# A different prologue for a one-core kernel: one load of the input, constants in two loads, the weights' low part on VectorE

## The chip, the cores and the metric

The kernel runs on one core of one Trainium2 chip. The metric is the device time of one execution in microseconds (us), as the median of several runs.

## The reference

The input `x` is 8 images of 64 channels of 16x16 pixels in float32. Two blocks follow each other, each added to its input:

```
g = group_norm(x)                              # 32 groups of 2 channels, per image
offsets = conv3x3(g, off_w) + off_b            # 8 heads x 9 taps x 2
aw = sigmoid(conv3x3(g, attn_w) + attn_b)      # 8 heads x 9 taps
v = Wv g
sampled = bilinear(v at pixel + tap + offset)  # 4 corners, zero outside
x = x + Wo * sum_taps(sampled * aw)
h = group_norm(x)
p_gn = group_norm(conv3x3(top_pool(relu(conv3x3(h, p1))) + left_pool(relu(conv3x3(h, p2))), p_w))
x = x + relu(conv3x3(relu(p_gn + group_norm(conv1x1(h, c1_w))), c2_w) + c2_b)
```

Only the start of the first block, up to its offset and attention convolutions and its values, is touched by the change.

## The kernel before

Every engine has a hand-written program that runs in its own order, and semaphores tie them together. The prologue goes like this.

- Loads. SP issues the first four images to `x_b` (partitions 0 to 63), all constants to `cst`, the convolution weights `w_off` to the lower half of `w_raw` (it shares its memory with `prod`, the name that the trace shows), the eight images once more to `x_t` (all eight on partitions 0 to 63), then biases, value weights and small vectors. ACT's queue issues images 4 to 7 to the upper half of `x_b`, and `w_off` to the upper half of `w_raw`.
- Statistics. VectorE (DVE) takes mean and variance of each channel from `x_b` (L586 to L592). TensorE (PE) joins the two channels of a group with two matrices out of `cst` (L917; it waits for the whole of `cst`). DVE makes the variances (L598 to L600), GpSimd (POOL) raises them to the power -0.5 (L374), and DVE makes the shifts (`affine`, L609).
- The normalised input. `g_t` gets the eight images out of `x_t`: five by DVE (L702), three by ScalarE (ACT, L418).
- Splitting. Float32 products are made from rounded parts: `g_pair` holds the rounded input on partitions 0 to 63 and the same, one column on, on 64 to 127; `g_cross` holds the rest of the rounding on the lower half and the rounded input on the upper. This is done in three ranges of columns: DVE writes `g_pair` (L709) and `g_cross` (L711), ACT copies both to the upper half (`copy_high`, L426 and L427). The weights are split in the same way: `w_pair` by DVE (L716, queued behind the first range) and ACT (L432, queued behind the first `copy_high`), `w_cross` by ACT (L412) with its upper half then reduced to the low part by POOL (L382), and the bias row by ACT (L430) and POOL (L387).
- The convolutions. The 16 columns of the image are worked on in chunks of 2, 4, 4, 4 and 2 (`CHUNKS`). `conv_column` makes one column by 6 matmuls of `g_pair` (L958), 9 of `g_cross` (L964), and one for the bias (L966). PE makes chunk 0, then all values (`values`, L939), then chunk 1, and then the rest between its other work. Until its input is there PE is kept busy by 20 matmuls that nobody reads (`keep_warm`, L924), which start behind the statistics.
- Behind it, ACT copies offsets out of PSUM (L449), makes the interpolation weights (`distances`, `hats`), and copies the values out (`copy_values`, L439). DVE multiplies (L768, L733, L760). PE sums (L979, L1004). From chunk 0 on the same pattern repeats for each chunk, and the second block follows.

Of the kernel before, what the change touches and what calls it, by code (L numbers as in the profile page):

```python
# [70 lines left out]
BETWEEN = (3, 2, 2, 0, 0)  # L71
WARM_START, WARM_CHUNK = 20, (0, 0, 0, 16, 10)
WARM_IN = (11, 14)
# [12 lines left out]

C_GB = 0
C_GT = C_GB + P
C_RAMP = C_GT + 2 * P
C_ID = C_RAMP + 2 * W - 1  # L90
# [16 lines left out]
def build(nc, x, consts, w_off, w_v, off_bias, w_o, w12, b12, wp, wc1, wc2, vecs, out):  # L107
    with ExitStack() as ctx:
# [90 lines left out]
        ld_x = [sem(f"ld_x{i}") for i in range(2)]  # L199
        ld_xt = sem("ld_xt")  # L200
        ld_cst = sem("ld_cst")
        ld_w0 = [sem(f"ld_w0_{i}") for i in range(4)]
        ld_w12, ld_wp, ld_vec, ld_c = sem("ld_w12"), sem("ld_wp"), sem("ld_vec"), sem("ld_c")
# [105 lines left out]
        def _(sp):  # L309
            sp.dma_start(x_b[lo, :, :], x_d[0:HALF].rearrange("n c p -> c n p")).then_inc(ld_x[0], 16)  # L310
            sp.dma_start(cst[:, :], consts).then_inc(ld_cst, 16)
            sp.dma_start(w_raw[lo], w_off).then_inc(ld_w0[1], 16)
            sp.dma_start(x_t[:, :, :], x_d.rearrange("n c p -> c n p")).then_inc(ld_xt, 16)
            sp.wait_ge(bias_zero, 1)
            for row in (0, LO_ROW):
                sp.dma_start(bias_s[row:row + 1, :], off_bias).then_inc(ld_w0[2], 16)
            for rows in (lo, hi):
                sp.dma_start(w_v_s[rows, :], w_v).then_inc(ld_w0[0], 16)
            sp.dma_start(w_o_s[:, :], w_o).then_inc(ld_w0[3], 16)
            sp.dma_start(vec_s[:, :], vecs).then_inc(ld_vec, 16)  # L320
            sp.dma_start(b12_s[:, :], b12).then_inc(ld_vec, 16)
# [39 lines left out]
        @block.gpsimd  # L361
        def _(pool):
            nc.gpsimd.memset(ones[:, :], 1.0).then_inc(zeroed, 1)
            nc.gpsimd.memset(bias_s[:, :], 0.0).then_inc(bias_zero, 1)
            nc.gpsimd.memset(half_pow[:, :], -0.5)
            nc.gpsimd.memset(g_pair[:, PW - 1, :, :].bitcast(F32), 0.0)
            nc.gpsimd.memset(ones_r[:, :].bitcast(F32), 1.0)
            nc.gpsimd.memset(w_v_pair[:, :].bitcast(F32), 0.0)
            nc.gpsimd.memset(w_pair[:, 1::2, :].bitcast(F32), 0.0).then_inc(zeroed, 1)
            nc.gpsimd.memset(v[:, :, :, :], 0.0).then_inc(v_zero, 1)  # L370

            def rstd(s, cols):
# [4 lines left out]
            pool.wait_ge(zeroed, 2)  # L377
# [24 lines left out]
        DVE_IMAGES = 5  # L402

        @block.scalar
        def _(act):
# [8 lines left out]
            act.wait_ge(ld_xt, 16)  # L414
            act.wait_ge(g_zero, 1)
            act.wait_ge(norm_ready, 1)
            for n in range(DVE_IMAGES, N):
                nc.scalar.activation(g_t[:, 1:W + 1, 1:H + 1, n].rearrange("p x y -> p y x"), rows_cols(x_t[:, n, :]),  # L418
                                     ACT.Identity, bias=ab[lo, G0, 3, n:n + 1],
                                     scale=ab[lo, G0, 2, n:n + 1]).then_inc(g_ready, 1)  # L420

# [9 lines left out]
            copy_high(0)  # L431
            nc.scalar.activation(w_pair[hi, 0::2, :], w_raw[hi, 1::KS, :], ACT.Copy).then_inc(w_high, 1)  # L432
            copy_high(1)
# [10 lines left out]
            def copy_offsets(c):  # L444
                x0 = CHUNKS[c][0]
                act.wait_ge(off_ps, c + 1)
                for b, k in enumerate(CONV_BANKS[c]):
# [123 lines left out]
        def _(ve):  # L571
# [123 lines left out]
            norm_stats(G0, [x_b[:, n, :] for n in range(HALF)])  # L695
            variance(G0, N, bank[7][:, 0:2 * N])
            affine(G0, N)
            ve.wait_ge(norm_ready, 1)
            ve.wait_ge(ld_xt, 16)
            ve.wait_ge(g_zero, 1)  # L700
            for n in range(DVE_IMAGES):
                nc.vector.tensor_scalar(g_t[:, 1:W + 1, 1:H + 1, n].rearrange("p x y -> p y x"),  # L702
                                        rows_cols(x_t[:, n, :]), ab[lo, G0, 2, n:n + 1], ab[lo, G0, 3, n:n + 1],
                                        ALU.mult, ALU.add).then_inc(g_ready, 1)

            ve.wait_ge(g_ready, N)
            ve.wait_ge(zeroed, 2)
            for r, (xa, xb) in enumerate(RANGES):
# [201 lines left out]
        def _(pe):  # L910
# [33 lines left out]

            def conv_column(c, j):

# [6 lines left out]
                if c and j == (2 if c == 1 else 0):  # L953
                    pe.wait_ge(u_ready, c)
                ps = bank[CONV_BANKS[c][j // 2]][:, (j % 2) * NCH:(j % 2 + 1) * NCH]
                for t in range(2 * KS):
                    ky, single = t // 2, t % 2
                    nc.tensor.matmul(ps, g_pair[:, x + 2 * single, ky:ky + H, :].rearrange("p y n -> p (y n)"),  # L958
                                     w_pair[:, t, :], start=(t == 0), stop=False)
                if c == 0 and j == 0:  # L960
                    pe.wait_ge(w_split, 2)
                for t in range(K2):
                    ky, kx = t // KS, t % KS
                    nc.tensor.matmul(ps, g_cross[:, x + kx, ky:ky + H, :].rearrange("p y n -> p (y n)"),  # L964
                                     w_cross[:, t, :], start=False, stop=False)
                last = nc.tensor.matmul(ps, ones_r[:, :], bias_r[:, :], start=False, stop=True)  # L966
                if j == CHUNKS[c][1] - 1:
                    last.then_inc(off_ps, 1)

            def tap_sum(c, g):  # L970
# [62 lines left out]
            pe.wait_ge(v_ready, 1)  # L1033
# [156 lines left out]
```

## Time and profile before

| | |
|---|---|
| median of 3 runs | 163.49 us (161.29 to 163.99) |
| the profiled execution's own time | 164.37 us |
| its span, first to last instruction | 162.5 us |
| mean granted TensorE clock, as a share of 2.4 GHz | 0.964 |
| busy: PE, DVE, ACT, POOL | 80%, 69%, 36%, 14% of the span |
| chain that ended last: PE, DVE, issue, DMA, ACT | 48%, 26%, 10%, 7%, 5% |

The profile's first line of each engine gives its busy share, and the chain of work that ended last says which of that work set the end. An engine may be busy and off that chain. The span leaves out 1.87 us of the execution's own time (164.37 less 162.5).

### The profile page before, as it was taken

Reading aid. Unit: us, or ns where it says so; the run is one execution under the profiler, and the core shown is the slowest. Engines: PE = TensorE matmul, PEld = TensorE weight load, DVE = VectorE, ACT = ScalarE, POOL = GpSimd, SP = SyncE. Lnnn points to the kernel's source line nnn. Section 1 sums busy time; section 2 is a strip of 40 time slices with the busy share of each in tenths; the row PEclk is TensorE's granted clock in tenths of the full one; section 3 lists DMA queues with packets and bytes.
Section 4 is the critical chain, followed back from the end, with each engine's and each line's share of the span. In section 5 each row is a group of like instructions: output and inputs, shape, how many; then the busy total and the mean of one; then the engine's idle time right before and its main releaser. Section 6 shows DMA issues by size and latency. Waiting matters only on the chain.

```text
span 162.5 us, 3252 instructions
## 1 busy us (share of the span) xinstructions
PE 130.0 (80%) x1387; PEld 110.9 (68%) x1387; DVE 112.7 (69%) x195; ACT 59.2 (36%) x107; POOL 22.4 (14%) x27
## 2 busy tenths in 40 slices
PE   0069109999899899999999998998689996685790
PEld 0057009999799789999899886886476564453560
DVE  5515997059148999699969999985580596857611
ACT  3009058660990469007962054020010415103301
POOL 8817900000000000000035000000010101020100
PEclk9999955999999999999999999999978999999998
DMA  4991000009963000000000000000000000000014
GB/s 127 246 188 28 0 0 0 4 0 257 237 128 78 0 2 4 0 0 4 0 0 0 4 0 0 0 0 6 2 0 4 0 6 4 0 4 0 0 36 97
DMA packets 7058, 5.96 MB, mean 37 GB/s; under 512 B 4656, under 2 KB 6194, under 8 KB 7042
## 3 DMA queue, kind: packets, MB, share of 16 engines
q1 hardware_dynamic: 6370, 4.71, 12.6%
q10 hardware_dynamic: 672, 1.02, 2.5%
q8 instruction: 11, 0.18, 0.5%
q14 instruction: 5, 0.04, 0.1%
HBM read 3.31 MB, written 0.52 MB: 24 GB/s over the span
## 4 chain that ended last, share of the span: by engine, by line
PE 48%; DVE 26%; issue 10%; DMA 7%; ACT 5%; SPq 1%; POOL 1%; POOLq 0%; DVEq 0%
PE bank L964 9%; PE bank L979 9%; PE bank L1004 7%; PE bank L958 7%; DMA x_t<-in_x 7%; DVE prod L733 6%; PE bank L924 4%; DVE part L760 3%; DVE x_t L859 3%; PE bank L1095 3%; PE bank L1128 3%; PE bank L939 2%; DVE wy L768 2%; DVE g_t L702 2%; DVE pooled L865 1%
## 5 line engine op out<-in xcount | busy, mean ns | idle before, releaser
L760 DVE TENSOR_TENSOR part<-v,bank 128x1280 f32<-128x1280 f32 (+3 forms) x20 | 21.5, 1111 | 9.7 <-PE bank L1004 4.3
L733 DVE TENSOR_TENSOR prod<-hat,wy 128x1440 f32<-128x1440 f32 (+3 forms) x25 | 27.3, 1158 | 0.0
L979 PE MATMUL bank<-cst,prod 128*128 128x128 f32 (+3 forms) x189 | 22.3, 272 | 0.8 <-DVE prod L733 0.8
L979 PEld LDWEIGHTS bank<-cst,prod 128*128 128x128 f32 (+3 forms) x189 | 20.7, 132 | 1.4 <-DVE prod L733 1.0
L1004 PE MATMUL bank<-cst,part 128*128 128x128 f32 x168 | 20.9, 274 | 0.8 <-issue 0.4
L924 PE MATMUL bank<-ones_r 128*128 128x512 f32 x71 | 20.8, 452 | 0.0
L958 PE MATMUL bank<-w_pair,g_pair 128*128 128x216 f32 x96 | 15.0, 294 | 7.0 <-ACT w_pair L432 7.0
L1004 PEld LDWEIGHTS bank<-cst,part 128*128 128x128 f32 x168 | 18.3, 140 | 2.1 <-DVE part L760 1.8
L964 PE MATMUL bank<-w_cross,g_cross 128*128 128x216 f32 x144 | 19.6, 283 | 0.0
L964 PEld LDWEIGHTS bank<-w_cross,g_cross 128*128 128x128 f32 x144 | 18.3, 201 | 0.0
L958 PEld LDWEIGHTS bank<-w_pair,g_pair 128*128 128x128 f32 x96 | 12.8, 202 | 7.7 <-ACT w_pair L432 7.4
L924 PEld LDWEIGHTS bank<-ones_r 128*128 128x128 f32 x71 | 15.2, 220 | 3.4
L374 POOL TENSOR_TENSOR ab<-ab,half_pow 128x2 f32<-128x2 f32 (+1 forms) x7 | 5.8, 834 | 64.5 <-DVE ab L600 64.5
L917 PE MATMUL bank<-mv,cst 128*128 128x4 f32 (+1 forms) x16 | 3.3, 289 | 13.5 <-DMA cst<-in_consts 9.7
L464 ACT ACTIVATE hat<-u 128x576 f32<-128x576 f32 (+1 forms) x25 | 13.7, 579 | 0.0
L917 PEld LDWEIGHTS bank<-mv,cst 128*128 128x128 f32 x16 | 2.7, 221 | 16.1 <-DMA cst<-in_consts 9.7
L449 ACT ACTIVATE u<-bank 128x432 f32<-128x432 f32 x8 | 3.9, 529 | 20.5 <-PE bank L966 20.5
L768 DVE TENSOR_TENSOR wy<-hat,mod 128x1440 f32<-128x1440 f32 (+1 forms) x5 | 6.8, 1352 | 6.6 <-ACT hat L474 6.6
L474 ACT ACTIVATE hat<-hat 128x2880 f32<-128x2880 f32 (+1 forms) x5 | 10.7, 2130 | 0.2
L1128 PE MATMUL bank<-g,wc_s 64*64 64x256 f32 x144 | 8.5, 379 | 2.8 <-DVE g L892 2.8
L482 ACT ACTIVATE cell_t<-bank 128x256 f32<-128x256 f32 (+5 forms) x15 | 4.8, 317 | 14.4 <-PE bank L979 14.3
L1115 PE MATMUL bank<-pooled,wp_s 64*64 64x256 f32 x144 | 8.6, 379 | 1.4 <-DVE pooled L865 1.4
(91 smaller groups left out, 166.5 us busy)
## 6 DMA issues: line engine op xcount, KB each, us to landing
v<-v SPq DMA_DIRECT2D x2, 480.0 KB, 6.3
v<-v SPq DMA_DIRECT2D x2, 448.0 KB, 5.8
x_t<-in_x SPq DMA_DIRECT2D x1, 512.0 KB, 10.9
prod<-in_w_off ACTq DMA_DIRECT2D x1, 486.0 KB, 7.5
prod<-in_w_off SPq DMA_DIRECT2D x1, 486.0 KB, 9.7
w_s<-in_w SPq DMA_DIRECT2D x4, 72.0 KB, 3.7
wc_s<-in_wc SPq DMA_DIRECT2D x2, 144.0 KB, 3.0
wp_s<-in_wp SPq DMA_DIRECT2D x4, 72.0 KB, 2.9
```

The lines of the kernel that those rows point to most:

```text
L464: nc.scalar.activation(hat[:, c % 2, d, 0:2 * ck].rearrange("p (k x h) -> p k x h", x=w, h=HEADS), u[:, 0:2 * K2, xs, :], ACT.Abs, bias=fl ...
L474: nc.scalar.activation(hat[:, c % 2, :, 0:2 * ck], hat[:, c % 2, :, 0:2 * ck], ACT.Relu, bias=1.0, scale=-1.0).then_inc(hat_ready, 1)
L733: return nc.vector.tensor_tensor(prod[:, 0:K2 * CELLS * cx].rearrange("p (k q s) -> p q k s", k=K2, s=cx)[:, q0:q0 + nd], hat[:, c % 2, d0 ...
L760: nc.vector.tensor_tensor(part[:, n % PARTS, 0:nd, 0:cv].rearrange("p d (q e) -> p d q e", e=HD), moved, weights.unsqueeze(3).to_broadcast ...
L768: made_wy = tick(nc.vector.tensor_tensor(wy[:, :, 0:ck].rearrange("p d (k q) -> p d k q", k=K2), hat[:, c % 2, :, ck:2 * ck].rearrange("p ...
L924: nc.tensor.matmul(ps.rearrange("p (a q) -> p a q", q=P), ones_r[:, :], ones_r[:, :].unsqueeze(1).to_broadcast([P, 4, P]), start=True, sto ...
L958: nc.tensor.matmul(ps, g_pair[:, x + 2 * single, ky:ky + H, :].rearrange("p y n -> p (y n)"), w_pair[:, t, :], start=(t == 0), stop=False)
L964: nc.tensor.matmul(ps, g_cross[:, x + kx, ky:ky + H, :].rearrange("p y n -> p (y n)"), w_cross[:, t, :], start=False, stop=False)
L979: last = nc.tensor.matmul(out_ps[0:size, b * P:(b + 1) * P], prod[:, at:at + size], ident, start=(b == 0 and t == 0), stop=(b == n - 1 and ...
L1004: last = nc.tensor.matmul(comb_bank[:, j * P:(j + 1) * P], part[:, n % PARTS, d, j * P:(j + 1) * P], ident, start=(m == 0 and d == 0 and j ...
L1115: last = nc.tensor.matmul(image(bank[P_BANK[g] + r][k * C:(k + 1) * C, 0:HW]), wp_s[rows, t, k, :], window(pooled, rows, g, t), start=(t = ...
L1128: last = nc.tensor.matmul(image(bank[OUT_BANK[g] + k][r * C:(r + 1) * C, 0:HW]), wc2_s[rows, t, :], window(g2, rows, DUO * g + r, t), star ...
```

## The change

- `x_t` isn't loaded any more. Both engines normalise out of `x_b`: images 0 to 3 from its lower half, 4 to 7 from its upper half, with the scales and shifts of the same partitions. DVE makes six images, ACT two.
- `cst` comes in two loads: the two matrices of the statistics first, the rest behind the value weights and `w_o`.
- POOL no longer makes the weights' low part. DVE does, behind the first range of `g_pair` and `g_cross`. DVE's two `w_pair` copies move ahead of `affine`, with a wait for both weight loads in front of them. ACT's `w_pair` copy moves ahead of its `w_cross` copy.
- POOL gets one small power operation ahead of the first real one. Its bias subtraction waits for ACT's third weight copy, and its `memset` of `wp_s` for both subtractions.
- PE gets 14 more matmuls that nobody reads (`WARM_LOAD`), ahead of the statistics, and 18 instead of 20 behind them. It makes the `g_pair` taps of both columns of chunk 0, each column in a bank of its own, then the `g_cross` taps of both, then two columns of chunk 1, then the values, then the other two columns. ACT copies chunk 0's offsets in two pieces.

```diff
-WARM_START, WARM_CHUNK = 20, (0, 0, 0, 16, 10)
+WARM_LOAD, WARM_START, WARM_CHUNK = 14, 18, (0, 0, 0, 16, 10)
...
-            sp.dma_start(cst[:, :], consts).then_inc(ld_cst, 16)
+            sp.dma_start(cst[:, 0:C_GB], consts[:, 0:C_GB]).then_inc(ld_gt, 16)
             sp.dma_start(w_raw[lo], w_off).then_inc(ld_w0[1], 16)
-            sp.dma_start(x_t[:, :, :], x_d.rearrange("n c p -> c n p")).then_inc(ld_xt, 16)
...
+            sp.dma_start(cst[:, C_GB:], consts[:, C_GB:]).then_inc(ld_cst, 16)
...
+            pool.wait_ge(zeroed, 2)
+            nc.gpsimd.tensor_tensor(pow_out[:, :], ones[:, :], half_pow[:, 0:1], ALU.pow).then_inc(pow_warm, 1)
...
-            pool.wait_ge(w_high, 1)
             pool.wait_ge(rstd_ready, 1)
-            nc.gpsimd.tensor_tensor(w_cross[hi, :, :], w_raw[hi], w_cross[hi, :, :].bitcast(F32),
-                                    ALU.subtract).then_inc(w_split, 1)
-            pool.wait_ge(w_split, 1)
-            pool.wait_ge(w_high, 2)
+            pool.wait_ge(w_high, 3)
...
-        DVE_IMAGES = 5
+        DVE_IMAGES = 6
+
+        def image_parts(n):
+            rows = (lo, hi)[n // HALF]
+            return (g_t[:, 1:W + 1, 1:H + 1, n].rearrange("p x y -> p y x"), rows_cols(x_b[rows, n % HALF, :]),
+                    ab[rows, G0, 2, n:n + 1], ab[rows, G0, 3, n:n + 1])
...
             act.wait_ge(ld_w0[1], 32)
+            act.wait_ge(zeroed, 2)
+            nc.scalar.activation(w_pair[hi, 0::2, :], w_raw[hi, 1::KS, :], ACT.Copy).then_inc(w_high, 1)
             nc.scalar.activation(w_cross[:, :, :], w_raw, ACT.Copy).then_inc(w_high, 1)
...
             variance(G0, N, bank[7][:, 0:2 * N])
+            ve.wait_ge(ld_w0[1], 32)
+            ve.wait_ge(zeroed, 2)
+            for kx, single in ((0, 0), (2, 1)):
+                nc.vector.tensor_copy(w_pair[lo, single::2, :], w_raw[lo, kx::KS, :]).then_inc(w_pair_ready, 1)
             affine(G0, N)
             ve.wait_ge(norm_ready, 1)
-            ve.wait_ge(ld_xt, 16)
...
                 if r == 0:
-                    ve.wait_ge(ld_w0[1], 32)
-                    for kx, single in ((0, 0), (2, 1)):
-                        nc.vector.tensor_copy(w_pair[lo, single::2, :], w_raw[lo, kx::KS, :]).then_inc(w_pair_ready, 1)
+                    ve.wait_ge(w_high, 2)
+                    nc.vector.tensor_tensor(w_cross[hi, :, :], w_raw[hi], w_cross[hi, :, :].bitcast(F32),
+                                            ALU.subtract).then_inc(w_split, 1)
...
-            pe.wait_ge(ld_cst, 16)
+            pe.wait_ge(zeroed, 2)
+            keep_warm(WARM_LOAD, bank[0][:, :])
+            pe.wait_ge(ld_gt, 16)
             group_means(G0, HALF, bank[7], (C_GT, C_GT + P))
-            pe.wait_ge(zeroed, 2)
             keep_warm(WARM_START, bank[0][:, :])
...
+            pe.wait_ge(w_high, 2)
+            pe.wait_ge(w_pair_ready, 2)
+            pe.wait_ge(ld_cst, 16)
+            for j in range(CHUNKS[0][1]):
+                pair_taps(0, j)
             pe.wait_ge(w_high, 3)
-            pe.wait_ge(w_pair_ready, 2)
-            for c in range(2):
-                for j in range(CHUNKS[c][1]):
-                    conv_column(c, j)
-                if c == 0:
-                    values()
+            pe.wait_ge(w_split, 2)
+            for j in range(CHUNKS[0][1]):
+                cross_taps(0, j)
+            conv_column(1, 0)
+            conv_column(1, 1)
+            values()
+            conv_column(1, 2)
+            conv_column(1, 3)
```

## Rows read from the trace of the kernel before

**Rows 1.** The chain that ended last, 13 to 45 us: start us, us, what.

```profile
18.48 2.77 DVE g_t L702 x4
...
24.03 1.62 PE bank L958 x6
25.64 1.92 PE bank L964 x9
...
29.66 3.53 PE bank L939 x32
33.19 0.71 PE bank L958 x6
33.90 1.00 PE bank L964 x9
```

**Rows 2.** Timeline, 0 to 24 us: start, us, engine, what, idle time ahead and its releaser.

```profile
1.99 5.44 POOL L370 MEMSET v<- 128x6400 f32 x1
...
7.23 0.16 DVE L592 TENSOR_TENSOR mv<-mv,sq 128x4 f32<-128x4 f32 x1
...
9.69 1.02 PE L917 MATMUL bank<-mv,cst 128*128 128x8 f32 x4 [9.69 <-DMA cst<-in_consts]
...
10.56 6.49 PE L924 MATMUL bank<-ones_r 128*128 128x512 f32 x20
...
11.47 1.64 POOL L374 TENSOR_TENSOR ab<-ab,half_pow 128x8 f32<-128x8 f32 x1 [4.04 <-DVE ab L600]
12.15 1.82 ACT L412 ACTIVATE w_cross<-prod 128x1944 fp32r<-128x1944 f32 x1 [8.49 <-DMA prod<-in_w_off]
...
13.93 2.02 ACT L418 ACTIVATE g_t<-x_t,ab 64x256 f32<-64x256 f32 x3
13.99 7.25 DVE L702 TENSOR_SCALAR g_t<-x_t,ab 64x256 f32<-64x256 f32 x5 [0.67 <-DMA x_t<-in_x]
14.05 4.34 POOL L382 TENSOR_TENSOR w_cross<-prod,w_cross 64x1944 fp32r<-64x1944 f32 x1 [0.94 <-ACT w_cross L412]
15.75 0.38 ACT L430 ACTIVATE bias_r<-bias_s 128x216 fp32r<-128x216 f32 x1
18.47 0.63 POOL L387 TENSOR_TENSOR bias_r<-bias_s,bias_r 1x216 fp32r<-1x216 f32 x1
19.16 1.18 POOL L390 MEMSET wp_s<- 128x1152 f32 x1
21.28 0.53 DVE L709 CAST g_pair<-g_t 64x720 fp32r<-64x720 f32 x1
...
22.66 1.10 DVE L716 CAST w_pair<-prod 64x648 fp32r<-64x648 f32 x2
23.24 0.74 ACT L432 ACTIVATE w_pair<-prod 64x648 fp32r<-64x648 f32 x1
```

**Rows 3.** Timeline, last stretch of DVE's images, 20.85 to 21.3 us.

```profile
20.44 0.80 DVE L702 TENSOR_SCALAR g_t<-x_t,ab 64x256 f32<-64x256 f32 x2
```

**Rows 4.** DMA issues: KB each, us from issue to landing.

```profile
cst<-in_consts SPq DMA_DIRECT2D x1, 271.5 KB, 8.1
```

**Rows 5.** Windows of the prologue: busy (count) by engine, granted clock, DMA share, GB/s.

```profile
2.00:8.00 6.00, 0.00 (x0) 0.00 (x0) 3.68 (x11) 1.49 (x2) 5.43 (x2) 1.00 0.97 246
20.00:21.00 1.00, 0.00 (x0) 0.00 (x0) 1.00 (x3) 0.00 (x0) 0.34 (x1) 1.00 0.00 0
21.00:22.00 1.00, 0.00 (x0) 0.00 (x0) 0.93 (x3) 0.16 (x1) 0.00 (x0) 0.50 0.00 0
```

**Rows 6.** The page's groups: busy us, mean ns, idle ahead.

```profile
L374 POOL TENSOR_TENSOR ab<-ab,half_pow 128x2 f32<-128x2 f32 (+1 forms) x7 | 5.8, 834 | 64.5 <-DVE ab L600 64.5
```

**Rows 7.** Groups of 0 to 34 us, shapes kept apart: DVE's longest `g_cross` subtraction.

```profile
L711 DVE TENSOR_TENSOR g_cross<-g_t,g_pair 64x1296 fp32r<-64x1296 f32 x1 | 1.5, 1503 | 0.0
```

**Rows 8.** DVE's waits, 34 to 60 us: total us, times, longest.

```profile
DVE part L760 <- PE bank L992: 3.6, 1, 3.6
```

**Rows 9.** Timeline, DVE's first work on the interpolation weights.

```profile
34.29 0.91 DVE L768 TENSOR_TENSOR wy<-hat,mod 128x720 f32<-128x720 f32 x1 [6.63 <-ACT hat L474]
```

More of the change, by code:

```diff
@@ L84 @@
 G0, G_IN, G_C1, G_P, NORMS = 0, 1, 3, 5, 7
-C_GB = 0
-C_GT = C_GB + P
-C_RAMP = C_GT + 2 * P
+C_GT = 0
+C_GB = C_GT + 2 * P
+C_RAMP = C_GB + P
 C_ID = C_RAMP + 2 * W - 1
@@ L146, in build @@
         warm = sb("warm", [P, 1])
+        pow_out = sb("pow_out", [P, 1])
         vfar = part[:, :, :, :].rearrange("p b d s -> p (b d s)")[:, 0:VW * C].rearrange("p (x c) -> p x c", c=C)
@@ L199, in build @@
         ld_x = [sem(f"ld_x{i}") for i in range(2)]
-        ld_xt = sem("ld_xt")
+        ld_gt = sem("ld_gt")
         ld_cst = sem("ld_cst")
+        pow_warm = sem("pow_warm")
         ld_w0 = [sem(f"ld_w0_{i}") for i in range(4)]
@@ L375, in rstd @@
                                         ALU.pow).then_inc(rstd_ready, 1)
-            pool.wait_ge(zeroed, 2)
             rstd(G0, N)
-            pool.wait_ge(w_high, 1)
             pool.wait_ge(rstd_ready, 1)
-            nc.gpsimd.tensor_tensor(w_cross[hi, :, :], w_raw[hi], w_cross[hi, :, :].bitcast(F32),
-                                    ALU.subtract).then_inc(w_split, 1)
-            pool.wait_ge(w_split, 1)
-            pool.wait_ge(w_high, 2)
+            pool.wait_ge(w_high, 3)
             row = slice(LO_ROW, LO_ROW + 1)
@@ L411, in _ @@
             act.wait_ge(ld_w0[1], 32)
+            act.wait_ge(zeroed, 2)
+            nc.scalar.activation(w_pair[hi, 0::2, :], w_raw[hi, 1::KS, :], ACT.Copy).then_inc(w_high, 1)
             nc.scalar.activation(w_cross[:, :, :], w_raw, ACT.Copy).then_inc(w_high, 1)
-            act.wait_ge(ld_xt, 16)
             act.wait_ge(g_zero, 1)
@@ L417, in _ @@
             for n in range(DVE_IMAGES, N):
-                nc.scalar.activation(g_t[:, 1:W + 1, 1:H + 1, n].rearrange("p x y -> p y x"), rows_cols(x_t[:, n, :]),
-                                     ACT.Identity, bias=ab[lo, G0, 3, n:n + 1],
-                                     scale=ab[lo, G0, 2, n:n + 1]).then_inc(g_ready, 1)
+                to, image, scale, shift = image_parts(n)
+                nc.scalar.activation(to, image, ACT.Identity, bias=shift, scale=scale).then_inc(g_ready, 1)
             def copy_high(r):
@@ L431, in _ @@
             copy_high(0)
-            nc.scalar.activation(w_pair[hi, 0::2, :], w_raw[hi, 1::KS, :], ACT.Copy).then_inc(w_high, 1)
             copy_high(1)
@@ L446, in copy_offsets @@
                 act.wait_ge(off_ps, c + 1)
-                for b, k in enumerate(CONV_BANKS[c]):
+                if c == 0:
+                    for j in range(2):
+                        last = nc.scalar.activation(u[:, :, x0 + j, :],
+                                                    bank[1 + j][:, j * NCH:(j + 1) * NCH].rearrange(
+                                                        "p (k h) -> p k h", h=HEADS), ACT.Copy)
+                for b, k in enumerate(CONV_BANKS[c] if c else ()):
                     xa = x0 + 2 * b
@@ L696, in _ @@
             variance(G0, N, bank[7][:, 0:2 * N])
+            ve.wait_ge(ld_w0[1], 32)
+            ve.wait_ge(zeroed, 2)
+            for kx, single in ((0, 0), (2, 1)):
+                nc.vector.tensor_copy(w_pair[lo, single::2, :], w_raw[lo, kx::KS, :]).then_inc(w_pair_ready, 1)
             affine(G0, N)
             ve.wait_ge(norm_ready, 1)
-            ve.wait_ge(ld_xt, 16)
             ve.wait_ge(g_zero, 1)
             for n in range(DVE_IMAGES):
-                nc.vector.tensor_scalar(g_t[:, 1:W + 1, 1:H + 1, n].rearrange("p x y -> p y x"),
-                                        rows_cols(x_t[:, n, :]), ab[lo, G0, 2, n:n + 1], ab[lo, G0, 3, n:n + 1],
-                                        ALU.mult, ALU.add).then_inc(g_ready, 1)
+                to, image, scale, shift = image_parts(n)
+                nc.vector.tensor_scalar(to, image, scale, shift, ALU.mult, ALU.add).then_inc(g_ready, 1)
             ve.wait_ge(g_ready, N)
-            ve.wait_ge(zeroed, 2)
             for r, (xa, xb) in enumerate(RANGES):
@@ L943, in values, with column_ps, pair_taps @@
                 last.then_inc(v_ps, 1)
-            def conv_column(c, j):
+            def column_ps(c, j):
+                if c == 0:
+                    return bank[1 + j][:, j * NCH:(j + 1) * NCH]
+                return bank[CONV_BANKS[c][j // 2]][:, (j % 2) * NCH:(j % 2 + 1) * NCH]
+            def pair_taps(c, j):
                 x = CHUNKS[c][0] + j
@@ L954, in conv_column, with cross_taps @@
                     pe.wait_ge(u_ready, c)
-                ps = bank[CONV_BANKS[c][j // 2]][:, (j % 2) * NCH:(j % 2 + 1) * NCH]
                 for t in range(2 * KS):
                     ky, single = t // 2, t % 2
-                    nc.tensor.matmul(ps, g_pair[:, x + 2 * single, ky:ky + H, :].rearrange("p y n -> p (y n)"),
+                    nc.tensor.matmul(column_ps(c, j), g_pair[:, x + 2 * single, ky:ky + H, :].rearrange("p y n -> p (y n)"),
                                      w_pair[:, t, :], start=(t == 0), stop=False)
-                if c == 0 and j == 0:
-                    pe.wait_ge(w_split, 2)
+            def cross_taps(c, j):
+                x = CHUNKS[c][0] + j
                 for t in range(K2):
                     ky, kx = t // KS, t % KS
-                    nc.tensor.matmul(ps, g_cross[:, x + kx, ky:ky + H, :].rearrange("p y n -> p (y n)"),
+                    nc.tensor.matmul(column_ps(c, j), g_cross[:, x + kx, ky:ky + H, :].rearrange("p y n -> p (y n)"),
                                      w_cross[:, t, :], start=False, stop=False)
-                last = nc.tensor.matmul(ps, ones_r[:, :], bias_r[:, :], start=False, stop=True)
+                last = nc.tensor.matmul(column_ps(c, j), ones_r[:, :], bias_r[:, :], start=False, stop=True)
                 if j == CHUNKS[c][1] - 1:
                     last.then_inc(off_ps, 1)
+            def conv_column(c, j):
+                pair_taps(c, j)
+                cross_taps(c, j)
             def tap_sum(c, g):
```

## Prediction

> **What bounds the kernel now.** I read the chain of work that ended last first, then the timeline of its first 24 us, because the change touches nothing behind that. The chain [rows 1] hangs on DVE's images until 21.24 us, then on the copies that follow them, and from 24.03 us on PE's columns and values. PE is thus late for one reason: its operand isn't there. The timeline [rows 2] shows why. The images begin at 13.99 us, when the second copy of the input lands, and five of them take 7.25 us. The last two take 0.80 together, 0.40 each [rows 3]; five would be 2.0. The other 5.2 us coincide with POOL: its weight subtraction runs from 14.05 to 18.39, then a bias subtraction of 0.63 and a `memset` of 1.18. DVE's image waits behind each of them. ACT, beside the same POOL operations, makes three images in 2.02 us. So 4.3 us of the path are a subtraction of POOL's for which nobody is waiting until much later.
>
> The Trainium skill has this as a rule ("SBUF — State Buffer", section "Who interferes with whom"): copies, casts and `tensor_scalar` of VectorE can use the port pair that it shares with GpSimd, and whichever engine starts second is blocked for the whole instruction. By that rule the trace agrees: the first image lasts as long as POOL's subtraction. It names casts too, so the `w_pair` copies below would be held up beside POOL, which is the case that I take; without the rule it would be rival (a).
>
> **Loads.** The first half of the columns' delay goes with `x_t`. The two weight loads now land at 12.15 us [rows 2], behind 271.5 KB of constants [rows 4] and beside 512 KB of `x_t`. After the change 512 (input), 128 (constants) and 972 KB (weights) have to come, 1651 thousand bytes. At the 246 GB/s of [rows 5], which start at 2 us, that takes 6.7 us and ends at 8.7; with some half us for the landing I take 9.3 us. It can't be earlier than 8.7, and 12.15 is the upper bound if nothing is won. The first constants stand behind the same input as now and are less than half as large: the bounds are 4.7 us (640 KB at 246 GB/s) and 9.7 (now, 8.1 after the issue, [rows 4]). I take 7.3, between them; PE needs them when the statistics are ready, at 7.39 [rows 2]. The rest of the constants is asked for much later, but PE needs it no sooner than about 15 us.
>
> **Statistics.** PE's four small matmuls take 1.02 us [rows 2], until about 8.4 instead of 10.71. Then DVE's variances (PE done at 10.71, POOL starts at 11.47: 0.75) let POOL start near 9.15. POOL's power operation took 1.64 us for 8 columns, while the six later ones with 2 columns took (5.8 - 1.64) / 6 = 0.70 each [rows 6]. Either the columns or the first call cost the 0.9 us. The added small one stands behind the `memset` of `v` (until 7.43) and takes between 0.5 and 1.6, by the same two readings. If the columns cost it, the real one runs from 9.1 to 10.7; if the first call does, the small one ends at 9.1 and the real one runs until some 10.3. Both give about 10.5 us, against 13.11 now.
>
> **Weights on DVE.** The two `w_pair` copies (1.10 us, [rows 2]) now stand ahead of `affine`, with the wait for the weights in front. Queued behind them are the shifts and all images, and ACT's images wait for the shifts too. If they don't collide with POOL, they run from 9.3 to 10.45, beside POOL's power operation, and cost nothing. But they are fast copies like those that POOL holds up in [rows 2, 3], and the power operation runs just then. Blocked by it, they run from 10.5 to 11.6. I take the blocked case, since the nearest rows (the images) were blocked at each of three POOL operations. Images then begin at about 11.95 instead of 13.99.
>
> **Images.** Six on DVE at 0.40 are 2.4 us, until 14.35. On ACT: `w_pair` 0.74 and `w_cross` 1.82 from 9.3 are done at 11.9, two images at 0.67 at 13.3, the bias copy of 0.38 at 13.7. Then POOL subtracts the bias (0.63), beside DVE's last image: it costs between 0 and 0.63, and I take 0.35. The reading from the upper half of the partitions I price at nothing; no row shows it with these operations, and the bound on the other side is the difference between 0.40 and 0.67 (ACT's rate) for two of DVE's, 0.5 us. Sum: `g_pair` begins at 14.7 instead of 21.28, 6.6 us earlier.
>
> **From there to PE.** ACT's `w_pair` copy (0.74, [rows 2]) no longer stands between the copies of the first range and the first matmul. PE starts 1.95 behind `g_pair` instead of 2.75: 0.8 us more. First column at 16.65 instead of 24.03, which is 7.4 us.
>
> The low part of the weights on DVE has 1944 elements. By the 1.50 us for 1296 [rows 7] it takes 2.25 us, and replaces the copies of 1.10 behind the first range, so the second range comes 1.15 later. Behind this instruction are queued the second and third range, for which ACT and PE wait. It begins 1.4 us behind `g_pair`'s start, as the copies did, and ends at +3.65. PE works meanwhile on two columns' pair taps, from +1.95 on, for 1.4 us at the full clock and 2.9 at the half [rows 1]: it waits 0.35 us or not at all. The second range is due when both columns are done, at 1.95 + 2 x 1.8 = +5.6. Its cast and ACT's two copies took 1.95 us for the larger first range, so it's there by +5.6. POOL's `memset` now waits for this subtraction and can hold up DVE's next cast by 1.18 at worst, some 0.9 of which PE would see. I take 0.3 for both, bounds 0 and 1.3.
>
> **Two columns ahead of the values.** ACT must finish the third range, whose cast comes 1.15 later than now, and then makes offsets and hats, which DVE waits for. DVE got them at 34.29 [rows 9], which is +13.0. There PE's offsets came last, at 29.66, 1.5 us behind ACT's copies; now they come at +5.6 and the copies at about +8.2, so +13.0 again. Two columns (3.6) and the values (3.53, [rows 1]) are done at +12.7, still before ACT turns to them. So their copy, and SP's moves of the rows, aren't delayed. In the half-clock case they are 1.9 us later, and the cover is DVE's own wait for PE in the first chunk, 3.6 us [rows 8]. This wait is also the reason why PE's lead is worth something further on: DVE was waiting for PE there, so it can follow. I let the whole lead pass to the end. The bounds for what DVE swallows are 0 and, if the first chunk's PE lead of some 2 us from the clock is lost entirely, 2.
>
> **Clock.** The first two columns ran at half clock: 1.62 + 1.92 us for 15 matmuls against 0.71 + 1.00 later [rows 1]. PE had stopped at 17.05; the granted clock was full in 20 to 21 us and half in 21 to 22 [rows 5], so it fell about 4 us behind the last matmul, and the half clock (1.2 of 2.4 GHz) cost about 2 us. Now the 18 filler matmuls start at 8.4. If the 14 ahead of them have brought PE to its full pace they end near 12.3, else near 14.2 (20 took 6.49, [rows 2]). PE is then idle 2.4 to 4.3 us before the first column. Whether the clock falls before or in the first columns I can't tell from that. Bounds 0 and 2, and I take a gain of 0.9, about half.
>
> **Sum.** 7.4 - 0.3 + 0.9 = 8.0 us. The profiled execution took 164.37, so 156.4; that one lay 0.9 above the median, and in terms of medians it's 155.5 us.
>
> **Rivals.**
> (a) *The casts don't collide.* `w_pair` is done at 10.45, images run from 10.8 to 13.2, `g_pair` starts at 13.35 and PE at 15.3, with an idle time of at most 3 us, so at full clock. Gain 8.7 + 2.0 - 0.8 (the wait for the low part) = 9.9: 153.6 us. For it speaks that only the images were seen blocked, never a cast. Against it, the casts are of the fast kind: 648 elements in 0.55 us, where the subtraction of [rows 7] takes 1.50 for 1296.
> (b) *Weights late, clock low.* They land at 10.5 to 12.15, since descriptors of the smaller loads share the engines. ACT's chain, 4.0 us from landing to its last image, puts `g_pair` at 14.9 to 16.5, PE at 16.9 to 18.5, with the half clock. Gain 5 to 6.5: 157 to 158.5 us.
> (c) *Gain swallowed.* The columns start as forecast, but its lead is used up because DVE, once its wait of 3.6 us is gone, sets the pace of the chunks, or images are held up by POOL as before. Gain 1 to 4: 159.5 to 162.5 us.
> (d) *Slower.* PE meets its first columns at the half clock and keeps it, because the pair taps are followed by a wait for `w_split` and small gaps. The six columns of 1.8 us and the values take 14.4 us at full clock, and before lost 2 us. At half clock throughout they lose 14.4, which is 12.4 more than before, less the 7.4: +5.0, 168.5 us. It turns the sign once the half clock has cost 9.4 us, that is has lasted 19 us. Against it: in [rows 1] PE came out of it within 3.7 us.
>
> **Chances.** Forecast 0.45, (a) 0.27, (b) 0.17, (c) 0.08, (d) 0.03. A change of this kernel's time within 2% (160.2 to 166.8) can't be told from none by the three runs, which spread over 2.7 us. Faster by more than 2%: 0.92; within: 0.05; slower: 0.03. The range goes from (a) with its bounds to the slow end of (b): 152.3 to 159 us.
>
> **What would show it.** `x_b` feeds the images and POOL's subtraction of 4.34 us is gone. DVE's `w_pair` copies last 1.1 us together if free, over 1.6 if blocked. Images start near 12, `g_pair` near 14.7, the first column near 16.7, and PE waits less than 0.5 us for the low part. The granted clock at 16 to 20 us tells whether the clock's term is there. The first chunk's waits of DVE for PE shrink, and behind 45 us everything stands about 8 us earlier. I'd be wrong if the weights landed past 11 us, if images reading the upper partitions took longer than 0.5 us each, or if DVE's second range came later than 6 us behind the first.

## The result and the profile after

The changed kernel takes 155.81 us (median of 4 runs, 154.91 to 156.15) against 163.41 us; the ratio is 0.956, with a 95% interval of 0.952 to 0.960. The forecast was 155.5 us, from 152.3 to 159.0. The profiled execution took 156.15 us with a span of 154.3, 8.2 less than before. An occasional execution takes 1.5 to 3% longer than the others of its kernel, at a lower granted clock; the comparisons below go by medians, and such an execution is named where a claim or a trace meets it.

I read the timeline of the changed kernel's start first, beside [rows 2] (start, us, engine, what, and in brackets the idle time ahead with what ended it).

```profile
1.99 5.43 POOL L372 MEMSET v<- 128x6400 f32 x1
...
7.47 0.56 POOL L374 TENSOR_TENSOR pow_out<-ones,half_pow 128x1 f32<-128x1 f32 x1
...
9.20 0.61 PE L926 MATMUL bank<-mv,cst 128*128 128x8 f32 x4 [0.96 <-DMA cst<-in_consts]
9.66 4.37 PE L933 MATMUL bank<-ones_r 128*128 128x512 f32 x18
...
10.50 1.74 POOL L378 TENSOR_TENSOR ab<-ab,half_pow 128x8 f32<-128x8 f32 x1 [2.48 <-DVE ab L608]
...
11.31 1.11 DVE L708 CAST w_pair<-prod 64x648 fp32r<-64x648 f32 x2 [0.89 <-DMA prod<-in_w_off]
12.08 1.84 ACT L418 ACTIVATE w_cross<-prod 128x1944 fp32r<-128x1944 f32 x1
...
12.53 2.38 DVE L714 TENSOR_SCALAR g_t<-x_b,ab 64x256 f32<-64x256 f32 x6
13.94 1.40 ACT L424 ACTIVATE g_t<-x_b,ab 64x256 f32<-64x256 f32 x2
...
15.37 0.53 DVE L718 CAST g_pair<-g_t 64x720 fp32r<-64x720 f32 x1 [0.47 <-ACT g_t L424]
15.89 0.63 POOL L386 TENSOR_TENSOR bias_r<-bias_s,bias_r 1x216 fp32r<-1x216 f32 x1 [3.65 <-ACT bias_r L434]
...
15.93 1.36 DVE L720 TENSOR_TENSOR g_cross<-g_t,g_pair 64x720 fp32r<-64x720 f32 x1
...
17.32 2.18 DVE L724 TENSOR_TENSOR w_cross<-prod,w_cross 64x1944 fp32r<-64x1944 f32 x1
17.54 2.37 PE L972 MATMUL bank<-w_pair,g_pair 128*128 128x216 f32 x12 [3.51 <-ACT g_cross L431]
19.53 1.39 DVE L718 CAST g_pair<-g_t 64x576 fp32r<-64x576 f32 x1
19.56 1.06 POOL L389 MEMSET wp_s<- 128x1152 f32 x1 [3.04 <-DVE w_cross L724]
...
29.63 0.91 DVE L777 TENSOR_TENSOR wy<-hat,mod 128x720 f32<-128x720 f32 x1 [5.17 <-ACT hat L482]
```

Six images of DVE's take 2.38 us, where five took 7.25, and nothing of POOL's is beside them. `g_pair` begins at 15.37 instead of 21.28, and PE's columns at 17.54 instead of 24.03, 6.5 us earlier. What binds has changed: DVE is done with its images at 14.91 and waits 0.47 us for ACT, whose chain begins with the weights at 11.31: 0.74 us for `w_pair`, 1.84 for `w_cross`, 1.40 for two images. The power operation of 8 columns takes 1.74 us although a small one ran ahead of it, and that one, with 1 column, took 0.56. So its time goes with the columns and not with the first call.

Half the clock is still there. These windows of the changed kernel show busy us by engine, the granted clock, DMA share and GB/s:

```profile
17.00:18.00 1.00, 0.46 (x4) 0.49 (x5) 0.97 (x2) 0.30 (x1) 0.00 (x0) 1.00 0.00 0
18.50:21.50 3.00, 3.00 (x16) 3.00 (x16) 2.93 (x3) 0.54 (x1) 1.06 (x1) 0.50 0.00 0
```

PE had been idle from 14.03 to 17.54, and the clock fell at about 18 us. The first 12 taps take 2.37 us instead of some 1.4. Thus the first two columns gained nothing from the clock.

The second block, in these two executions, did. The chain of the kernel before, in its second block, and then that of the changed kernel:

```profile
118.63 4.91 PE bank L924 x14
```

```profile
112.02 3.32 PE bank L933 x14
```

Up to these 14 fillers the changed kernel is 6.6 us ahead (118.63 - 112.02), behind them 8.2. A window of the kernel before shows why:

```profile
120.00:123.00 3.00, 3.00 (x9) 2.23 (x7) 1.98 (x9) 0.60 (x1) 0.01 (x1) 0.50 0.00 0
```

So 6.6 of the profile's 8.2 us come out of the prologue, and 1.6 are a fall of the clock that this execution of the kernel before had and the changed one's didn't.

### The profile page after: what moved, and what is told of

The parts are those of the page before. It is cut to its first block, busy times and chain, and to the rows that moved or that the text cites. A ratio compares the mean times of both kernels' runs of the same rounds, so it can differ in the third digit from the quotient of the medians.

```text
span 154.3 us, 3278 instructions
## 1 busy us (share of the span) xinstructions
PE 131.8 (85%) x1399; PEld 112.3 (73%) x1399; DVE 111.5 (72%) x197; ACT 59.0 (38%) x107; POOL 18.5 (12%) x27
## 4 chain that ended last, share of the span: by engine, by line
PE 49%; DVE 25%; issue 8%; ACT 6%; DMA 6%; POOL 1%; SPq 1%; POOLq 0%; DVEq 0%
PE bank L980 10%; PE bank L999 9%; PE bank L1024 8%; PE bank L972 7%; DVE prod L742 6%; DMA prod<-in_w_off 6%; PE bank L933 4%; DVE part L769 3%; DVE x_t L868 3%; PE bank L1122 3%; PE bank L1155 3%; PE bank L949 2%; DVE wy L777 2%; DVE pooled L874 2%; DVE bn L594 1%
## 5 line engine op out<-in xcount | busy, mean ns | idle before, releaser
L769 DVE TENSOR_TENSOR part<-v,bank 128x1280 f32<-128x1280 f32 (+3 forms) x20 | 21.5, 1111 | 7.8 <-PE bank L1024 4.3
L933 PE MATMUL bank<-ones_r 128*128 128x512 f32 x83 | 23.2, 436 | 2.1 <-POOL w_pair L371 2.1
L933 PEld LDWEIGHTS bank<-ones_r 128*128 128x128 f32 x83 | 17.0, 212 | 5.8 <-POOL w_pair L371 2.1
L457 ACT ACTIVATE u<-bank 128x432 f32<-128x432 f32 x7 | 3.4, 529 | 16.3 <-PE bank L982 16.3
L1155 PEld LDWEIGHTS bank<-g,wc_s 64*64 64x64 f32 x144 | 5.9, 132 | 4.9 <-ACT g L556 3.6
L1122 PE MATMUL bank<-g,w_s 64*32 64x256 f32 x288 | 8.7, 378 | 0.2 <-ACT g L529 0.2
```

The source lines that it names most:

```text
L769: nc.vector.tensor_tensor(part[:, n % PARTS, 0:nd, 0:cv].rearrange("p d (q e) -> p d q e", e=HD), moved, weights.unsqueeze(3).to_broadcast ...
L933: nc.tensor.matmul(ps.rearrange("p (a q) -> p a q", q=P), ones_r[:, :], ones_r[:, :].unsqueeze(1).to_broadcast([P, 4, P]), start=True, sto ...
L1122: last = nc.tensor.matmul(image(bank[R12_BANK[g] + r][cols, 0:HW]), w12_s[rows, t, b * CD:(b + 1) * CD], window(g1, rows, DUO * g + k, t), ...
L1155: last = nc.tensor.matmul(image(bank[OUT_BANK[g] + k][r * C:(r + 1) * C, 0:HW]), wc2_s[rows, t, :], window(g2, rows, DUO * g + r, t), star ...
```

## The experiments

**`a_pool_low`: POOL makes the low part again.**

```diff
-                if r == 0:
-                    ve.wait_ge(w_high, 2)
-                    nc.vector.tensor_tensor(w_cross[hi, :, :], w_raw[hi], ...).then_inc(w_split, 1)
+            pool.wait_ge(w_high, 2)
+            nc.gpsimd.tensor_tensor(w_cross[hi, :, :], w_raw[hi], ...).then_inc(w_split, 1)
```

> The changed kernel with one part undone: POOL makes the weights' low part again, behind ACT's rounded copy (done at 13.9 us), and DVE doesn't. Theory 1 (POOL's operation holds up DVE's images): POOL runs from about 13.95 to 18.3, the three images that DVE has left then wait for it, DVE's first g_pair starts near 19.5 instead of 15.37 and the kernel is 3.5 to 4.5 us slower. Theory 2 (the gain came from the earlier loads alone, and the images of the kernel before were slow for another reason): the images go on at 0.40 us each, g_pair starts at 15.4, the low part is there at 18.3 and is needed at 19.5, and without the 2.2 us of DVE's subtraction the kernel is the same or up to 0.5 us faster.

161.41 us (ratio to before 0.987, 0.980 to 0.994), 4.9 us above the changed kernel on that chip (156.54, below). Its timeline:

```profile
12.33 6.79 DVE L718 TENSOR_SCALAR g_t<-x_b,ab 64x256 f32<-64x256 f32 x6
...
13.86 4.31 POOL L385 TENSOR_TENSOR w_cross<-prod,w_cross 64x1944 fp32r<-64x1944 f32 x1 [1.81 <-ACT w_cross L422]
...
19.15 1.35 DVE L722 CAST g_pair<-g_t 64x720 fp32r<-64x720 f32 x1
```

The images take 4.4 us longer, as long as POOL's operation lasts, with all loads as in the changed kernel. That is theory 1. The 4.9 us are more than the 3.5 to 4.5 that it gave: `g_pair` comes 3.8 us later, its cast is then held up by the `memset` as well (1.35 instead of 0.53 us), and the half clock lasts longer (0.50 throughout 24 to 26 us, where the changed kernel has 1.00). Taking this part out costs 4.9 of the 7.6 us; the next run has it alone.

**`b_dve_low`: the kernel before with only the low part moved to DVE.**

```diff
+                    ve.wait_ge(w_high, 1)
+                    nc.vector.tensor_tensor(w_cross[hi, :, :], w_raw[hi], ...).then_inc(w_split, 1)
```

> The kernel before with one part of the change alone: DVE makes the weights' low part, behind its two w_pair copies, and POOL doesn't. Theory 1 (POOL's 4.3 us operation held the images up): the five images take about 2.6 us instead of 7.25, g_pair starts near 16.7 instead of 21.28, PE's first column near 19.5 instead of 24.03; PE then waits about 1 us for the low part and 1 us for the third range; 2.5 to 4 us faster than before. Theory 2 (half or more of the 8 us came from loads, order and clock): under 2 us faster.

160.46 us against 163.36 (0.986, 0.980 to 0.992): 2.9 us faster. Timeline:

```profile
13.87 1.84 DVE L698 TENSOR_SCALAR g_t<-x_t,ab 64x256 f32<-64x256 f32 x5 [0.74 <-DMA x_t<-in_x]
...
15.88 0.53 DVE L705 CAST g_pair<-g_t 64x720 fp32r<-64x720 f32 x1 [0.17 <-ACT g_t L414]
...
18.74 2.18 DVE L714 TENSOR_TENSOR w_cross<-prod,w_cross 64x1944 fp32r<-64x1944 f32 x1
18.81 0.90 PE L957 MATMUL bank<-w_pair,g_pair 128*128 128x216 f32 x6 [1.97 <-DVE w_pair L712]
...
20.97 1.40 PE L963 MATMUL bank<-w_cross,g_cross 128*128 128x216 f32 x5 [1.27 <-DVE w_cross L714]
```

`g_pair` comes 5.4 us earlier and PE's first taps 5.2, but only 2.9 are left. The low part now stands behind `w_pair` on DVE, PE does six taps and waits 1.27 us for it, and the later ranges stand behind it too. That the rest of the change (copies ahead of the images, both columns' pair taps first, two columns before the values) turns the freed time into gain is argued from these waits; of these parts only the last was run by itself, next.

**`a_values_first`: values directly behind chunk 0.**

```diff
+            values()
             conv_column(1, 0)
             conv_column(1, 1)
-            values()
```

> The changed kernel with the order of the columns undone: chunk 0, all values, then the four columns of chunk 1. Theory 1 (the two columns ahead of the values fill a wait): PE is done with chunk 0 at about 23 us, the values need the third range, which ACT has copied near 25, so PE stands idle 2 us, chunk 1's offsets come 2 us later, and so does all behind them: 1.5 to 2 us slower. Theory 2 (DVE has slack in the first chunk, 1.6 and 1.3 us, and takes up the delay; the values, 1.6 us earlier, let the rows move earlier): the same within 0.5 us.

158.19 us (0.969, 0.964 to 0.973), 1.65 us above the changed kernel on the same chip. Two of the five executions took 162.72 and 163.33 us, at clocks of 0.94, and the trace kept is the first of these; it serves only for the wait in PE's timeline, where the clock was nearly full (0.96 in 24 to 26 us):

```profile
24.65 0.30 PE L949 MATMUL bank<-w_v_pair,g_pair 128*128 128x128 f32 x1 [1.21 <-ACT g_cross L431]
```

This is theory 1: the values wait for the third range's copies (1.21 us here, 2 forecast), and DVE's slack doesn't take it up.

**`a_xt_load` and `a_late_small`: which loads delay the weights?** The first issues the dropped load again, the second holds the small loads back until the weights have landed.

```diff
+            sp.dma_start(x_t[:, :, :], x_d.rearrange("n c p -> c n p")).then_inc(ld_xt, 16)
```

> The changed kernel with the dropped load of 512 KB issued again behind the lower weights, where it was; nothing of the prologue waits for it. Theory 1 (the transfers share the engines, so what is queued behind the weights still delays them): the weights land near 12.1 instead of 11.29 us, ACT's chain of copies and images shifts by it, and the kernel is 0.7 to 0.9 us slower. Theory 2 (a load queued behind another one doesn't delay it): the weights land at 11.3 and the time is the same within 0.3 us; the earlier landing then came from the split of the constants.

```diff
             sp.wait_ge(bias_zero, 1)
+            sp.wait_ge(ld_w0[1], 32)
```

> The changed kernel, with SP waiting until both weight loads have landed before it issues the biases, the value weights, w_o, the rest of the constants and the small vectors. Theory 1 (the 2 us that the prediction had too little for the weights are these loads, 210 KB in small pieces, sharing the engines): the weights land at 9.3 to 10.3 us instead of 11.29, the first constants before 8.5 instead of 9.18, g_pair starts 0.8 to 1.5 us earlier, and the kernel is that much faster, unless the bias arrives later than the first matmuls need it. Theory 2 (the rate is bound by the large loads' own pieces): the weights land within 0.3 us of 11.29, and the later loads, which then land near 15 us, make the kernel the same or slower.

157.19 us (0.962, 0.956 to 0.968) and 156.50 us (0.956, 0.949 to 0.963). The weights' first reader in the one and in the other:

```profile
10.99 1.11 DVE L711 CAST w_pair<-prod 64x648 fp32r<-64x648 f32 x2 [0.99 <-DMA prod<-in_w_off]
```

```profile
11.00 1.11 DVE L709 CAST w_pair<-prod 64x648 fp32r<-64x648 f32 x2 [0.62 <-DMA prod<-in_w_off]
```

As to the landing, both refute theory 1: 512 KB behind the weights don't delay them, nor do the small loads. In all nine traces of the changed kernel and its variants with this order of loads the first reader goes between 10.68 and 11.31 us, with or without the `x_t` load; in the three with the constants in one load (`before`, `b_dve_low`, `b_warm`) between 11.76 and 12.15. That leaves the split of the constants as the likely cause of the earlier landing, which no run tests by itself. (That `a_xt_load` is 0.65 us slower decides nothing: this lies within the runs' spread, and in its trace the half clock lasts until past 23 us, in the changed kernel's until 21.5.) The windows of `a_late_small`, where nothing else is under way, show what stands between the bulk of the weights and their reader:

```profile
8.50:9.00 0.50, 0.00 (x0) 0.00 (x0) 0.00 (x0) 0.00 (x0) 0.00 (x0) 1.00 0.70 140
9.00:9.50 0.50, 0.36 (x4) 0.36 (x4) 0.00 (x0) 0.00 (x0) 0.00 (x0) 1.00 0.30 78
9.50:10.00 0.50, 0.50 (x5) 0.45 (x5) 0.17 (x1) 0.00 (x0) 0.00 (x0) 1.00 0.11 31
10.00:11.00 1.00, 1.00 (x6) 0.82 (x5) 0.34 (x3) 0.00 (x1) 0.55 (x1) 1.00 0.00 0
```

The bulk is over by 9 us, close to the 8.7 that bytes and rate gave. Then some of the 16 engines finish late, the last near 10, and the readers go at 11.00. From bulk to reader it's 2 us, where I had allowed 0.6. The Trainium skill ("DMA: Bandwidth & Descriptors", section "Anatomy of one DMA — SWDGE (gpsimd) path") gives some 2 us of fixed cost for a DMA issued through GpSimd, most of it behind the last byte. These loads are issued by SP and ACT, and the windows show 1 us behind the last byte and about 1 more for the uneven end.

**`a_warm30`: 30 fillers instead of 18.**

```diff
-WARM_LOAD, WARM_START, WARM_CHUNK = 14, 18, (0, 0, 0, 16, 10)
+WARM_LOAD, WARM_START, WARM_CHUNK = 14, 30, (0, 0, 0, 16, 10)
```

> The changed kernel with 30 filler matmuls behind the statistics instead of 18. They end near 16.6 instead of 14.03 us, 0.9 us ahead of the first column. Theory 1 (the first two columns run at half clock because PE stood idle for 3.5 us): granted clock 1.00 in 17.5 to 21.7 us, the 12 pair taps take 1.4 instead of 2.37 us, PE then waits for the low part until 19.5, and the first chunk is done about 1.5 us earlier; kernel 1.2 to 1.9 us faster. Theory 2 (the clock falls whatever the fillers are, or the low part and the second range come next and take the gain): less than 0.5 us.

156.19 us (0.955, 0.949 to 0.961): no gain that can be seen. Windows, and then the timeline:

```profile
18.00:19.00 1.00, 1.00 (x10) 0.82 (x8) 1.00 (x1) 0.00 (x0) 0.00 (x0) 1.00 0.00 0
```

```profile
17.44 1.57 PE L972 MATMUL bank<-w_pair,g_pair 128*128 128x216 f32 x12 [0.94 <-DVE g_cross L720]
...
19.43 1.40 DVE L718 CAST g_pair<-g_t 64x576 fp32r<-64x576 f32 x1
19.46 1.06 POOL L389 MEMSET wp_s<- 128x1152 f32 x1 [3.04 <-DVE w_cross L724]
19.54 1.23 PE L980 MATMUL bank<-w_cross,g_cross 128*128 128x216 f32 x9 [0.53 <-DVE w_cross L724]
```

Both theories were half right. The clock stays full here, with the fillers as the only edit, so the idle stretch was the cause of its fall. But PE, now faster, waits 0.53 us for the low part and then, 0.26 us, for the second range, which the `memset` has held up. Of some 1.9 us that the half clock costs in the two columns, 0.5 us are left at the end of chunk 1's columns (33.75 to 33.25). The traced execution (157.02 us) doesn't keep even that, because in the second block it has the fall of the clock that the changed kernel's trace was free of. Its chain there:

```profile
111.38 4.91 PE bank L933 x14
```

**`a_tuned`: three additions to the changed kernel.** The 30 fillers, 19 instead of 11 ahead of the second block's statistics, and the `memset` while DVE waits for PE.

```diff
-WARM_IN = (11, 14)
+WARM_IN = (19, 14)
...
             nc.gpsimd.tensor_tensor(pow_out[:, :], ones[:, :], half_pow[:, 0:1], ALU.pow).then_inc(pow_warm, 1)
+            nc.gpsimd.memset(wp_s[:, :, :, :], 0.0).then_inc(wp_zero, 1)
...
-            pool.wait_ge(w_split, 2)
-            nc.gpsimd.memset(wp_s[:, :, :, :], 0.0).then_inc(wp_zero, 1)
```

> The changed kernel with three additions: 30 fillers instead of 18 behind the statistics, 19 instead of 11 ahead of the second block's first statistics (both fill a stretch in which PE stands idle), and POOL's memset of wp_s moved from behind both subtractions to behind its first small power operation, where DVE waits for PE. Theory 1: the memset doesn't hold up DVE's second g_pair cast (0.44 instead of 1.39 us), the column behind chunk 0 starts at 21.9 instead of 22.8 us, the clock is full throughout, 0.99 or more in every run: 0.8 to 2 us faster than the changed kernel. Theory 2 (more fillers don't hold the clock; it falls in some executions of any kernel): the same time as the changed kernel, with clocks of 0.97 to 0.99.

154.84 us (154.43 to 154.99; 0.948, 0.944 to 0.952), 1.7 us below the changed kernel on the same chip (next run). The clock was 0.993 to 1.000. What each of the three additions gives by itself isn't shown. Its second cast, no longer held up:

```profile
19.47 0.45 DVE L717 CAST g_pair<-g_t 64x576 fp32r<-64x576 f32 x1
```

**`a_again`: the changed kernel once more, on the chip of the runs above.**

> The changed kernel itself, beside the other three on their chip. By every theory 155 to 156.5 us. What it adds is the spread of the granted clock: between 0.96 and 0.99 in its runs, with the half clock in 18 to 22 us in each of them if it's the idle stretch of PE that causes it.

156.54 us (0.956, 0.951 to 0.962). Three executions had clocks of 0.978 to 0.989, and one took 159.11 us at 0.967. The trace is of that one: the clock is 0.55 in 18 to 22 us and 0.60 in 22 to 26, and falls again in the second block (0.74 in 112 to 116).

**`b_warm`, `a_early_stats`, `a_tuned_again`: fillers in the kernel before, another order at the start, the three additions again.** They ran on another chip, where the kernel before took 162.88 us (12 executions, one of them 447.93). First `b_warm`:

```diff
-WARM_START, WARM_CHUNK = 20, (0, 0, 0, 16, 10)
-WARM_IN = (11, 14)
+WARM_START, WARM_CHUNK = 48, (0, 0, 0, 16, 10)
+WARM_IN = (19, 14)
```

> The kernel before with more fillers and nothing else: 48 instead of 20 behind its first statistics, 19 instead of 11 ahead of the second block's. Theory 1 (half clock costs the kernel before 2 us in its first two columns and, in some executions, 1.6 us in the second block): clock 0.99 or more, the first 15 matmuls in 1.8 instead of 3.5 us, 1.7 to 3.5 us faster than before; that much of the change's 7.3 us could have been had, or is left over, as clock. Theory 2 (PE's first columns are bound by the low part and the ranges, whatever the clock): under 1 us.

161.14 us (0.990, 0.986 to 0.994), clock 0.995 to 1.000 in all seven executions: 1.7 us, the lower end of theory 1. Fillers alone help the kernel before as much as fillers and the moved `memset` help the changed one. `a_early_stats`:

```diff
+            act.dma_start(cst[:, 0:C_GB], consts[:, 0:C_GB]).then_inc(ld_gt, 16)
             act.dma_start(w_raw[hi], w_off).then_inc(ld_w0[1], 16)
...
             affine(G0, N)
...                                     (images)
+            ve.wait_ge(ld_w0[1], 32)
+            ve.wait_ge(zeroed, 2)
+            for kx, single in ((0, 0), (2, 1)):
+                nc.vector.tensor_copy(w_pair[lo, single::2, :], ...).then_inc(w_pair_ready, 1)
```

> The changed kernel with the three additions (fillers in two places, the memset early), and the start in another order: the first constants come on ACT's queue ahead of the upper weights, the shifts and images stand ahead of the weight copies on both engines, and ACT's bias copy behind its first range. Theory 1 (the small load lags because it stands behind the lower input and shares turns with the large weight pieces; with it early, statistics are done at 8 instead of 9.8 us and the images fit in ahead of the weights' copies): first constants at 6 to 7.5 us, images from 11 us on, g_pair near 14.6 instead of 15.3, kernel 0.4 to 0.9 us faster than the one with the three additions. Theory 2 (the weights' landing at 11.1 us and the copies behind it bind): g_pair within 0.2 us of 15.3, the same time.

154.31 us (0.948, 0.944 to 0.952), the fastest median of all; one of the six executions took 157.84, at a clock of 0.977. `a_tuned_again`:

> The changed kernel with the three additions once more, beside the two others on their chip: 154.5 to 155 us with a clock of 0.99 or more in every run if the fillers hold it; a run at 0.98 or less would speak against that.

155.20 us (0.953, 0.949 to 0.958). Five of the six executions had clocks from 0.987 to 1.000, and one took 157.25 us at 0.978. A clock of 0.98 or less was to speak against the fillers: they hold it in most executions, not in all. The additions were worth 1.7 us where the changed kernel ran beside them. On this chip it didn't run, and the ratios (0.953 against 0.956) make it 0.5 us, with intervals that overlap. The timeline of `a_early_stats`:

```profile
8.09 0.51 PE L926 MATMUL bank<-mv,cst 128*128 128x8 f32 x4
...
11.19 2.40 DVE L709 TENSOR_SCALAR g_t<-x_b,ab 64x256 f32<-64x256 f32 x6
...
14.65 0.51 DVE L718 CAST g_pair<-g_t 64x720 fp32r<-64x720 f32 x1
...
16.13 2.18 DVE L724 TENSOR_TENSOR w_cross<-prod,w_cross 64x1944 fp32r<-64x1944 f32 x1
...
17.25 1.56 POOL L386 TENSOR_TENSOR bias_r<-bias_s,bias_r 1x216 fp32r<-1x216 f32 x1 [6.30 <-ACT bias_r L434]
```

`g_pair` begins at 14.65, the number of theory 1. But it does so on this chip without the new order too. The timeline of `a_tuned_again`, whose weights were read at 10.68 us:

```profile
14.76 0.53 DVE L717 CAST g_pair<-g_t 64x720 fp32r<-64x720 f32 x1 [0.48 <-ACT g_t L423]
```

So the new order moved `g_pair` by 0.1 us, and theory 2 is nearer: the traced executions are 0.3 us apart (154.26 and 154.55), and of the medians' 0.9 us, whose intervals overlap, the traces explain no more. What did move are the first constants. The DMA issues of the changed kernel and of this one (KB, us to landing) show how much their place matters:

```profile
cst<-in_consts SPq DMA_DIRECT2D x1, 128.0 KB, 7.6
```

```profile
cst<-in_consts ACTq DMA_DIRECT2D x1, 128.0 KB, 4.4
```

## Why the prediction was right

The main step was right, and the time with it, but the time by some luck. The changed kernel's prologue met rival (b)'s conditions: the weights landed late and the first columns ran at half clock. It gave 6.6 us, about the most that (b) had (6.5), and from the median of 163.49 that makes 156.9 us. The last 1.6 us of the profile came from the second block's clock, which the prediction hadn't looked at. One of its own signs of being wrong, weights past 11 us, came true.

- **POOL's subtraction as the cause** (4.3 us of the path): shown, by taking it away from the kernel before (images in 1.84 us) and by giving it back to the changed one (images 4.4 us longer).
- **The order of starts.** The prediction read [rows 2] as agreeing with the rule that it leaned on (last section). The durations agree. But there the image is recorded 0.06 us ahead of POOL's subtraction (13.99 and 14.05), and it was the image that was held up.
- **Images at 0.40 us, from the upper partitions too:** right, 2.38 us for six. ACT's chain from the weights to its last image was put at 4.0 and took 4.03.
- **The weights' landing** failed: 9.3 forecast, 11.31 measured at the first reader. Bytes and rate were right. The landing's "half us" was 2. And it wasn't the dropped `x_t` load that brought the weights forward: with it issued again they came no later. This made (b)'s mechanism the real one for `g_pair` (15.37, against 14.7 forecast and 14.9 to 16.5 in (b)).
- **The first constants** came at 9.2 instead of 7.3, and PE waited 0.96 us. That cost nothing, since the weights bound.
- **The casts blocked by POOL's power operation** failed: they run from 11.31 beside it (10.50 to 12.24) in 1.11 us, as before. Forecast were 10.5 to 11.6. The late weights, and no blocking, put them there.
- **0.8 us from ACT's `w_pair` copy:** 0.58, as 0.23 us pass between the copies' end and the first tap.
- **The low part, the second range and the `memset`** (0.3 us): in the changed kernel at half clock PE waited for none of them. The collision with the `memset` is real (1.39 instead of 0.44 us), and PE met it once the clock was full.
- **Two columns ahead of the values:** I had let PE's lead pass through at no cost, and it did, though not as reckoned. ACT's copies of the third range ended 9.6 us behind `g_pair` instead of 8.2, so DVE began on the interpolation weights 14.3 us behind it (29.63) instead of 13.0. ACT also waited 0.6 us for the values. DVE's wait for PE in the first chunk took it up and fell from 3.6 [rows 8] to 1.6 us. The order itself is worth 1.65 us.
- **The clock's term** (0.9 us, in the first columns): there it was 0.15 us. In the profiles 1.6 us came from the second block instead. That is a matter of the execution: `a_warm30` and `a_again` fell there too. On one chip, with more fillers in both (and the `memset` moved in the changed one), the kernel before took 161.14 and the changed one 155.20 us. So some 5.9 of the 7.6 us between medians are left when the clock is held nearly full.

So 7.4 - 0.3 + 0.9 was really 6.5 + 0.15 + 1.55. Rival (d) didn't come about: in the profile the half clock lasted some 3.5 us.

## What to carry to other kernels

When an instruction takes ten times its usual duration, look at what another engine runs in just that time: here one movable GpSimd subtraction cost VectorE 4.4 us. Moving it gave 2.9 us by itself, and the whole change, which also reorders what waits for the moved work, gave 7.6. For a load that something waits for, count bytes by the rate, and add the time from the bulk to the first reader as a trace of this kernel has it. Before crediting a change with a difference, compare the granted clock of each stretch in both profiles; fillers in idle stretches make the comparison, and the kernel, steadier in most executions.

## What the runs showed of the hardware that wasn't expected

- Whether POOL holds DVE up depends on its operation. A power operation of 8 columns on POOL (1.74 us) didn't delay two casts of DVE's in its midst, while a `memset` of POOL's made a cast take 1.39 instead of 0.45 us. The rule of the Trainium skill that the prediction leaned on ("SBUF — State Buffer", section "Who interferes with whom") says that the second to start is blocked for the whole instruction. In how long DVE is held, the `memset` and the subtractions agree, and the power operation doesn't. In who started first they don't: the cast that the `memset` held up is recorded 0.03 us ahead of it (19.53 and 19.56).
- It works in both directions: in `a_early_stats` POOL's subtraction of 0.63 us, begun 1.1 us into DVE's weight subtraction of 2.18, took 1.56.
- DVE's `g_cross` subtraction, with two inputs, took 1.36 instead of 0.90 us beside POOL's bias subtraction of 0.63.
- A load of 128 KB took 7.6 us to land on SP's queue, behind 256 KB and beside the large weight load on the other queue, and 4.4 us on ACT's queue, also behind 256 KB but ahead of that load.
